# Product keys: the pick weights of a pair's second tile are formed between two applications of the first tile's weights

## The reference, cut to what matters

```python
q = (xn @ w_q.T).reshape(b, n, 2, h, kd).transpose(2, 0, 1, 3, 4)
sim = jnp.einsum('pbnhd,hkpd->pbnhk', q, keys)
s, i = jax.lax.top_k(sim, k)
...
all_scores = (sx[..., :, None] + sy[..., None, :]).reshape(b, n, h, k * k)
all_idx = (ix[..., :, None] * nk + iy[..., None, :]).reshape(b, n, h, k * k)
scores, pk = jax.lax.top_k(all_scores, k)
idx = jnp.take_along_axis(all_idx, pk, axis=-1)
w_down = key_in[idx]
w_up = key_out[idx]
o = jnp.einsum('bnd,bnhkd->bnhk', inputs, w_down)
o = jax.nn.gelu(o, approximate=False) * jax.nn.softmax(scores, axis=-1)
return jnp.einsum('bnhk,bnhkd->bnd', o, w_up)
```

## Time and profile before

| what | us |
|---|---|
| median of 3 runs | 2040.0 |
| lowest and highest | 2035.83, 2042.59 |
| the profiled execution | 2041.42 |
| its span | 2039.7 |
| TensorE busy (matmul) | 1856.5 (91%) |
| VectorE busy | 1326.4 (65%) |
| ScalarE busy | 649.3 (32%) |
| GpSimd busy | 175.9 (9%) |
| mean granted TensorE clock | 0.953 |

### The profile page before, as it was taken

The page is one execution under the profiler, slowest core; times in us unless marked ns, Lnnn a source line. Parts: engine busy times, 40 slices in busy tenths (PEclk is TensorE's granted clock), DMA queues, the critical chain, the costliest instruction groups (busy, mean ns, idle before and its releaser), DMA issues. The chain is left out here.

```text
span 2039.7 us, 43767 instructions
## 1 busy us (share of the span) xinstructions
PE 1856.5 (91%) x16819; PEld 1549.4 (76%) x16819; DVE 1326.4 (65%) x3598; ACT 649.3 (32%) x1504; POOL 175.9 (9%) x125
## 2 busy tenths in 40 slices
PE   6999999699759999999999868878899999999998
PEld 5877787577548888888888735557688888888887
DVE  4555555377668888888788546656666665656564
ACT  3444344244421211221121024435433332333332
POOL 0000000111000000000000054631000000000000
PEclk9999999799879999999999969989899999999999
DMA  4000000221060000000000040001111111111101
GB/s 156 1 1 0 0 0 1 63 68 41 7 129 2 7 7 3 7 7 8 2 7 1 2 117 1 0 1 37 25 24 26 21 25 22 24 22 24 22 0 42
DMA packets 139320, 48.61 MB, mean 24 GB/s; under 512 B 108179, under 2 KB 138419, under 8 KB 139187
## 3 DMA queue, kind: packets, MB, share of 16 engines
q1 hardware_dynamic: 139186, 46.66, 10.2%
HBM read 42.43 MB, written 4.19 MB: 23 GB/s over the span
## 5 line engine op out<-in xcount | busy, mean ns | idle before, releaser
L2840 DVE TENSOR_TENSOR m_act_up<-m_silu,m_up 128x512 f32<-128x512 f32 x136 | 93.4, 687 | 168.4 <-PE m_up L587 125.3
L2759 ACT ACTIVATE m_silu<-m_gate 128x512 f32<-128x512 f32 x136 | 81.5, 599 | 380.0 <-PE m_gate L587 380.0
L2824 DVE SCALAR_TENSOR_TENSOR g_x<-m_y,m_combine,g_x 128x256 f32<-128x256 f32 x272 | 118.8, 479 | 53.0 <-PE m_y L587 51.4
L233 ACT ACTIVATE a_prob<-a_score,a_neg_max 128x128 f32<-128x128 f32 x256 | 90.6, 367 | 170.2 <-DVE a_neg_max L223 170.2
L2404 PE MATMUL f_out<-f_ko,f_gel 128*128 128x256 f32 x512 | 128.4, 404 | 0.9 <-DVE f_gel L2580 0.7
L2447 ACT ACTIVATE f_gel<-f_act 128x512 f32<-128x512 f32 x128 | 76.6, 599 | 132.3 <-PE f_act L587 90.9
L2404 PEld LDWEIGHTS f_out<-f_ko,f_gel 128*128 128x128 f32 x512 | 100.3, 203 | 15.9 <-issue 1.5
L2404 PE MATMUL f_turn<-f_ko,f_gel 128*128 128x256 f32 x512 | 111.8, 379 | 0.0
L587 PE MATMUL f_act<-f_hT_pair_high,f_kiT_high 128*128 128x256 f32 x384 | 108.2, 282 | 0.0
L2404 PEld LDWEIGHTS f_turn<-f_ko,f_gel 128*128 128x128 f32 x512 | 97.3, 190 | 13.2
L587 PE MATMUL f_act<-f_hT_pair_low,f_kiT_high 128*128 128x256 f32 x384 | 107.3, 279 | 0.0
(11 more groups left out here) (381 smaller groups left out, 5022.7 us busy)
## 6 DMA issues: line engine op xcount, KB each, us to landing
f_gel<-in_L_ffn_key_in SPq DMA_DIRECT2D x16, 256.0 KB, 4.8
f_ko<-in_L_ffn_key_out SPq DMA_DIRECT2D x2, 2048.0 KB, 18.4
g_shared<-in_ctx SPq DMA_DIRECT2D x8, 256.0 KB, 2.7
fp_wq_nat<-in_L_ffn_w_q SPq DMA_DIRECT2D x8, 256.0 KB, 3.1
h_kept<-fp_hT SPq DMA_DIRECT2D x8, 256.0 KB, 2.9
g_shared<-h_kept SPq DMA_DIRECT2D x8, 256.0 KB, 3.4
g_ctx_next<-in_ctx SPq DMA_DIRECT2D x8, 256.0 KB, 2.7
g_ctx_all<-in_ctx SPq DMA_DIRECT2D x1, 2048.0 KB, 10.4
```

What stands on the lines that cost most here:

```text
L233: last = act.activation(self.prob[:, u % 4, j, :], self.score_bank[u % 2][:, j // 2, (j % 2) * P:(j % 2 + 1) * P], ACT.Exp, bias=self.neg_ ...
L2759: act.activation(silu[:, m, :], gate_bank[m][:, :], ACT.Silu).then_inc(silu_ready[m].sem, 1)
L2824: last = dve.scalar_tensor_tensor(x[:, tile, :], y_bank[n][:, t * D:(t + 1) * D], weight, x[:, tile, :], ALU.mult, ALU.add)
L2840: dve.tensor_tensor(act_up[:, m, :], silu[:, m, :], up_bank[m][:, :], ALU.mult) \
```

## The change

`choose` is cut in two. Its last part, from the wait for `weight_exp` on, becomes `weigh`. For the tile 0 of each pair `weigh` is called right behind `choose`, as it stood. For tile 1 it is called from `apply_weights` of tile 0, after the application of group 0 and before that of group 1.

```diff
                     dve.tensor_tensor(codes[:, 0, d, :], high[:, 0, :], index[:, 0, :], ALU.add)
                     dve.tensor_copy(codes[:, 1, d, :], high[:, 1, :])
+
+            def weigh(chain, i, t):
+
+                if not exists(i):
+                    return
+                n = 2 * i + t
                 dve.wait_ge(weight_exp, n + 1)
                 chain.link(dve, dve.tensor_reduce(weight_sum[:, :], weight[:, :, :], AX.X, ALU.add))
...
-            def apply_weights(i, t):
+            def apply_weights(i, t, after=lambda m: None):
...
                                                  ALU.mult, ALU.mult).then_inc(g_used[q].sem, 1)
+                    after(m)
...
             choose(first_links, 0, 0)
+            weigh(first_links, 0, 0)
             for i in pairs_but_last(dve):
                 links.begin(i)
                 one_hot(links, i, 0)
                 choose(links, i, 1)
-                apply_weights(i, 0)
+                apply_weights(i, 0, lambda m: weigh(links, i, 1) if m == 0 else None)
                 one_hot(links, i, 1)
                 apply_weights(i, 1)
                 residual(i, 0)
                 choose(links, i + 1, 0)
+                weigh(links, i + 1, 0)
                 residual(i, 1)
```

## The result

The changed kernel takes 2010.5 us (median of 4 runs, 2009.4 to 2015.2) against 2040.6 (4 runs, 2035.8 to 2042.6). The ratio is 0.9867, with a 95% interval of 0.985 to 0.9884: 1.3% faster, some 9 us more than was forecast. In the profiled executions the span went from 2039.7 to 2009.8 us, 29.9 less.

What follows compares the result with a forecast made beforehand. It took TensorE as the bound, standing 16.2 us for VectorE's GELU applications. Terms A to D, 14.0 + 8.3 - 2.0 + 1.2 = 21.5 us, took the 2040.0 median to 2018.5, stated as 2019; range 2009 to 2030.

Steps and rivals of the forecast that it cites:

- The cover: On VectorE, application 0 fits into the 1.50 us idle before ScalarE's exponential ends; pick weights start as before, scalings keep 1.44.
- Term A: TensorE's group 2 starts 2.00 us earlier in each of seven pairs: 14.0 us saved.
- Term B: The stretch from group 2 to tile 1's first group shrinks to 15.52 us in seven pairs: 8.3 us saved.
- piece (a): Group 3 starts 2.00 us after group 2; its instruction block arrives 3.63 us after group 2's start, following a 0.9 break.
- (b): Group 3's last 14 matmuls, then similarities to first output at full clock: 0.30 and 1.49, reaching 5.42 us after group 2.
- (c): The first 46 output matmuls on TensorE take 10.10 us at full clock.
- Term C: Allowance for one fall of TensorE's clock in the seven pairs, 1.44 us standstills being harmless: 2.0 us lost.
- Term D: In the last pair, VectorE's applications and so the outputs come one application earlier, clock left alone: 1.2 us saved.
- No break: Rival, 6%: group 3's instruction block is asked for early enough, 0.9 us more saved in each of seven pairs: 2012.
- The block does not move: Rival, 10%: block requested before group 2's wait lands as now, TensorE stands later instead, no change: 2039.
- clock falls all the same: Rival, 8%: TensorE's clock still falls in every pair, only Term A and Term D stay: 2025.
- slower: Rival, 6%: block does not move, the 2.9 us standstill puts all half-clock time onto similarities and outputs: 2053.

Runs made afterwards that it cites:

- experiment 7: The kernel before, with one unused VectorE reduction of 1024 elements ahead of tile 0's application 0, holding group 2 longer: 2045.1 us, ratio 1.0032.
- experiment 8: The changed kernel, with two unused VectorE reductions of 1024 elements ahead of tile 0's application 0: 2024.8 us, ratio 0.9926.
- experiment 1: The changed kernel, with tile 1's pick weights formed behind the application of group 1 instead of group 0: 2006.4 us, ratio 0.9845.
- experiment 2: The changed kernel, with tile 1's pick weights formed behind all four applications: 2020.2 us, ratio 0.9911.
- experiment 6: The changed kernel, with ScalarE's rounding behind the next pair's first exponential, which moves GpSimd's subtraction: 2009.4 us, ratio 0.9855.
- experiment 9: experiment 1 with seven unused matmuls added in the last pair only, to fill TensorE's standstills there: 2006.7 us, ratio 0.9836.
- experiment 10: The changed kernel with the moves of experiment 1 and experiment 6 together: 2010.2 us, ratio 0.9851.
- experiment 4: The kernel before, with 18 matmuls added ahead of the loop, moving the instruction block's edge by 36 instructions: 2033.1 us, ratio 0.9979.
- experiment 3: The kernel before, with eight unused matmuls filling TensorE's standstill ahead of tile 0's group 2: 2022.9 us, ratio 0.9926.

## Why the prediction was right in its direction and too small

**The cover.** Right to within 0.02 us. Application 0 was to end at 0.01 us before the exponential and did so 0.01 after it (695.14, 695.13); the pick weights start 0.02 us later, and the scalings take 1.44 us.

**Term A.** Right: 2.00 us in each pair, 14.0 in all.

**Term B, piece (a), the step that failed.** The forecast gave the block 3.63 us "from the new start" of group 2. In the kernel before, application 0's end, the release of the wait and group 2's start lie within 0.14 us of each other, so its rows can't tell which of them the block is tied to. In the changed kernel they lie 1.3 us apart, and the packets pass at group 2's start instead of 0.9 us after it. With experiments 7 and 8, where they follow the release by 1.1 us whether it is later or earlier, this shows that the request waits for the release and not for group 2's matmuls. Taken from application 0's end, the 3.77 us of the rows before would have put the block at 699.43 + 3.77 = 703.20, ahead of the 50th matmul of group 3 at 703.44: no break. It was only just in time: in the changed kernel group 3 takes 1.01 us instead of 0.97, and in experiments 1, 2, 6, 9 and 10, whose group 3 starts 0.2 us earlier, TensorE halts behind the same 50th matmul in two to five of the seven pairs, by 0.1 to 0.4 us. No break gives 7 x 0.9 = 6.3 us. The rest of piece (a) was right: group 3 starts 2.00 us after group 2.

**Pieces (b) and (c).** The first 46 output records take 10.10 us, as forecast. The stretch without a break was bounded at 15.52 - 0.9 = 14.62 and is 14.50 in the mean, 0.9 us less in seven pairs. The same bound by its other half, `f_out` held to 705.1 by application 3, gives 705.1 - 700.74 + 10.10 = 14.46, and application 3 is indeed what ends last ahead of the outputs.

**Term C.** Not needed. With neither standstill nor break there is no fall in any pair: 2.0 us. So 6.3 + 0.9 + 2.0 = 9.2, the whole of the difference between 15.5 and 8.3 - 2.0. For the case that it assumed, its size was near: experiment 8 has the break and 0.84 us of standstill, and the clock falls in two of seven pairs, 1.2 us each. But its ground, that 1.44 us was harmless and 1.73 us was not, was chance in one execution: over twelve, falls follow the two in six and in seven.

**Term D.** Half right. The last pair's outputs start 7.04 us after its group 0 instead of 8.25, the 1.2 that were forecast. The fall still comes, as was assumed, but its price was not left alone. It begins 6.2 us after group 0 in both kernels, and as the outputs now start earlier, 6.0 us of it lie on them instead of 4.8 (1105.28 to 1111.2; 1135.92 to 1140.7). They take 13.04 instead of 12.47, and 0.64 us is left.

**The rivals.** *No break*, at 6%, is what happened. Its 2012 still had the one fall of term C; without it 2010, as measured. That this agrees so well is partly luck: the 0.9 us of the shorter stretches and the 0.6 us missing in term D nearly cancel. Against it I held that the break shows although TensorE had stood for 1.93 us. That was read the wrong way round. With a wait just ahead of the edge, the standstill is what brings the break: the sequencer waits too, and cannot come to the request. Where the request lies ahead of the wait, TensorE stands for 1.93 us without a break (experiment 4). *The block does not move* is refuted by the changed kernel's own packets (3.3 to 3.6 us behind group 0 instead of 6.5) and by experiment 7, and *clock falls all the same* by the trace; *slower* needed the former. As to the Trainium skill's rule ("Runtime: NRT & Kernel Launch", instruction fetch mechanics), that the next block is fetched while the current one is executed and that this is mostly hidden: the trace agrees where the request lies ahead of the wait (experiments 3 and 4, no break in seven pairs) or the wait is released early (the changed kernel, none in seven). Where the wait stands between, it is hidden only if the wait is released some 3.8 us before the block is needed (3.4 to 4.1 us in the pairs with a break). That its matmuls can lag the sequencer fits the Trainium skill's figure of 64 for TensorE's queue ("TensorE: Matmul & The Clock Gate", table of specifications); no run here measured the depth.

The range, 2009 to 2030, held the result near its lower end, whose case ("no break, no fall") is the one that came, but for the last pair's clock, which was to be better and was not. The forecast had given that case 6%.

## What to carry to other kernels

An instruction that waits for one engine and has nothing to do with the next one in its queue should not stand ahead of work that a third engine needs: look for an idle time on the engine that feeds the bottleneck, and move finished inputs into it. A standstill of TensorE has a price behind it that may be larger than itself (here 14.0 us of standing and 15.5 behind it, in falls of the clock and breaks of the instruction stream), and in the loop's seven pairs it went as a whole once the standstill went. When a delay is carried over to a moved instruction, ask to which of the events that coincide now it is tied.

## What the runs showed of the hardware

The break in the instruction stream: a block's packets pass 1.0 to 1.2 us after the wait ahead of it is released (1.6 and 1.7 us in one pair each of experiments 8 and 7), and the engine goes on 2.2 to 2.8 us after the packets, whether the wait ended 1.1 us later (experiment 7) or 1.1 us earlier (experiment 8) than before. Moving the edge by 36 instructions took the break away and left the standstill (experiment 4).

The granted clock after a standstill of TensorE, in the loop's seven pairs:

| kernel | standing in a pair, us | pairs with a fall |
|---|---|---|
| changed kernel, experiment 3 | none over 0.2 | 0 |
| experiment 2 | some 1.2 in one piece | 1 |
| experiment 8 | 0.84, then 0.54 to 0.89 | 2 |
| experiment 4 | 1.93 | 5 |
| before | 1.93, then up to 1.1 | 7 |
| experiment 7 | 3.06, then up to 0.63 | 7 |

In these rows it is a matter of more or less, with no sharp bound between 1.2 and 1.9 us, and each row is one execution. What decides in a single case stays open. The two standstills of the first stages bear this out: 1.44 us was followed by a fall in 6 of 12 executions, 1.73 us in 7 of 12. In the last pair, in several pieces, 1.0 and 2.0 us in sum were followed by none (experiments 9 and 3) and 2.3 us or more by a fall in every kernel. In the loop a fall lasted 3.4 us (0.8 to 1.3 us of time lost) or 6.8 us (2.1 to 2.3, breaks left out).

An operation of VectorE on two SBUF inputs took 1.44 us beside GpSimd's subtraction and 0.36 without it (experiments 1 and 6), 1.08 us for one instruction.
